# Moving VectorE's product of aggregate and x, and tying it to GpSimd's first scatter, in a graph kernel

## The chip, the cores and the metric

The kernel runs on one core of a Trainium2 chip, as one launch. The metric is the device time of the whole program in microseconds. The engines are named as the profile names them: PE (TensorE), DVE (VectorE), ACT (ScalarE), POOL (GpSimd) and SP (SyncE, which here only issues transfers).

## What is computed

Two graph layers run over 100,000 nodes of 64 features and 50,000 edges sorted by destination, each with a residual and a layer norm.

```
def L0(x):   messages = x[src] * edge_weight[:, None]
             agg = segment_sum(messages, dst, N)
             out = leaky(x * agg @ W1 + b1) + leaky(agg @ W2 + b2)      # leaky: slope 0.2
             return out * rsqrt(max(sum(out * out), 1e-12))
def L1(x):   messages = ffn(x[dst]; W1p, b1p, W2p, b2p) * edge_weight[:, None]
             agg = segment_sum(messages, src, N)
             out = ffn([x, agg]; W1u, b1u, W2u, b2u)                    # ffn: two layers, each with an exact gelu
             return out * rsqrt(max(sum(out * out), 1e-12))
x = layernorm(x + L0(x)); x = layernorm(x + L1(x))
```

## The kernel before

The work is done in three blocks, one after another: `first_edges`, `second_edges` and `last_rows`. The change is in the second.

The first block gathers x by source, weighs and joins the messages, and adds them into a table in device memory. A row of this table holds aggregate, x and centred x of a node.

The second block runs 98 rounds for nodes and edges together. In a round it takes one chunk of 1024 nodes (8 rows of 64 features in each partition), and one window of 512 edges (4 further rows, gathered from the table by destination). All 12 rows of a partition lie in one tile, `box`, of which there are six. DVE's `multiply` (L731) forms x times aggregate in place: both inputs are slices of `box` in SBUF, 128 partitions by 768 numbers. PE turns the rows (L570) and multiplies by the weights (L579), ACT writes the sloped branch (L658), and DVE's `leak` (L737) takes the larger branch, in three steps q = 0, 1, 2 for each chunk. PE's `outputs` (L589) forms the centred outputs, ACT squares them (L664), DVE sums the squares (L746), takes inverse roots by a chain of short instructions (L754 to L768), scales (L772) and adds the rows (`add_rows`, L780). ACT squares the sum (L669), DVE sums those squares (`sum_centred`, L742), and one round later DVE normalizes (L785). The neighbour rows then go through the message network on PE and ACT. PE's `join` (L625) weighs and sums the messages of a window, and ACT's `take` (L691) copies them into one of three tiles `ms`.

POOL does nothing in this block but issue indirect transfers. For each window k it issues four scatters, which add `ms` into `state` in device memory (L546), and then four gathers of window k + 8 into `box` (L532). Scatter k waits until window k is taken and until all four transfers of scatter k - 1 have landed. `take` of window i waits until the scatters of window i - 3 have landed, because they read the same `ms` tile. A gather of window i waits until `add_rows` has released the tile `box` of window i - 6.

SP issues, once a round, the load of the next chunk (768 KB, after `add_rows` has released its tile), the load of the join weights (640 KB) and the store of a finished chunk (256 KB), in that order.

Each engine has its own order, written out by hand as a loop over rounds t. `of(t, lag, f)` calls f for index t - lag. DVE's order, with ACT's lags one higher for the same index, is the one that matters:

```
for t in range(ROUNDS):
    of(t, 2, sum_outputs)
    ...
    of(t, 1, leak, 1)
    of(t, 2, add_rows)
    of(t, 1, leak, 2)
    of(t, 2, sum_centred)
    of(t, 0, multiply)
```

DVE's instructions start in this order and none passes another.

Of the kernel before, what the change touches and what calls it, by code (L numbers as in the profile page):

```python
# [28 lines left out]
def wait(eng, sem, n):  # L29

    if n > 0:
        eng.wait_ge(sem, n)  # L32
# [7 lines left out]
def gnn_kernel(nc, x, src, dst, edge_weight, w1a, w2a, b1a, b2a, w1p, b1p, w2p, b2p, w1u, b1u, w2u, b2u, out):  # L40
# [42 lines left out]
    with ctx:  # L83
# [6 lines left out]
        def sem(name, c=ctx):  # L90
            return c.enter_context(nc.semaphore(name))
# [350 lines left out]
        def second_edges():  # L442
            c = ExitStack()
            with c:
# [28 lines left out]
                scattered = [sem(f"scattered1_{h}") for h in range(HALVES)]  # L473
# [3 lines left out]
                    "squared", "summed_o", "squared_y", "summed_y", "guarded", "chain", "scaled", "added", "normed", "spread"))  # L477
                nt_up, nt_in, mixed, gelu1, mixed2, gelu2, summed, taken, preset = (sem(f"{q}1") for q in (
                    "nt_up", "nt_in", "mixed", "gelu1", "mixed2", "gelu2", "summed", "taken", "preset"))
                ROUNDS = NWIN + 6  # L480
                SPARE = R // 2 * M8

# [10 lines left out]
                with nc.Block(no_gpsimd_drain=True) as block:  # L493
                    @block.sync
                    def _(sp):
                        def load(i):

                            s = i % SB
                            wait(sp, added, i - SB + 1)
                            rows, p, g = chunk(table_rows, i)  # L500
                            sp.dma_start(box[s][0:p, WT:WT + g, :, :].rearrange("p g a f -> p g (a f)"),
                                         rows.rearrange("(g p) f -> p g f", g=g)).then_inc(loaded[s], 16)

                        def load_join(i):
                            wait(sp, summed, i - SW + 1)
                            sp.dma_start(weigh[i % SW][:, :].rearrange("p (b f) -> p b f", f=P), joins[i].rearrange("b p f -> p b f")).then_inc(joined[i % SW], 16)

                        def store(i):
                            sp.wait_ge(normed, i + 1)
                            rows, p, g = chunk(state_rows[:, 0, :], i)  # L510
                            sp.dma_start(rows.rearrange("(g p) f -> p g f", g=g), y[i % SY][0:p, WT:WT + g, :]
                                         ).then_inc(stored[i % SY], 16)

                        for i in range(NWIN + 7):
                            if i < NWIN:
                                load(i)
                            if 0 <= i - 6 < NWIN:
                                load_join(i - 6)
                            if 0 <= i - 7 < NWIN:
                                store(i - 7)  # L520
                        for s in range(SY):
                            sp.wait_ge(stored[s], 16 * lies(NWIN, s, SY))

                    @block.gpsimd
                    def _(pool):
                        def gather(i, h):

                            if h == 0:
                                wait(pool, added, i - SB + 1)
                            for b in range(JOIN * h, JOIN * (h + 1)):  # L530
                                at = i * WT + b
                                pool.indirect_dma_start(out=box[i % SB][:, b, :, :].rearrange("p a f -> p (a f)"), out_offset=None,  # L532
                                                        in_=table_rows[:, :],
                                                        in_offset=bass.IndirectOffsetOnAxis(ap=node[1][:, at:at + 1], axis=0),
                                                        ).then_inc(gathered[i % SB], 16)

                        def scatter(k, h):

                            if h == 0:
                                pool.wait_ge(taken, k + 1)  # L540
                                wait(pool, scattered[HALVES - 1], 16 * JOIN * k)
                            else:
                                pool.wait_ge(scattered[h - 1], 16 * JOIN * (k + 1))
                            for b in range(JOIN * h, JOIN * (h + 1)):
                                at = k * WT + b
                                pool.indirect_dma_start(out=state[:, :], out_offset=bass.IndirectOffsetOnAxis(ap=sidx[1][:, at:at + 1], axis=0),  # L546
                                                        in_=ms[k % SM][:, b, :], in_offset=None, compute_op=ALU.add,
                                                        ).then_inc(scattered[h], 16)

                        for i in range(LEAD):  # L550
                            for h in range(HALVES):
                                gather(i, h)
                        for k in range(NWIN):
                            for h in range(HALVES):
                                scatter(k, h)
                                if k + LEAD < NWIN:
                                    gather(k + LEAD, h)
                        for h in range(HALVES):
                            pool.wait_ge(scattered[h], 16 * JOIN * NWIN)

                    @block.tensor
                    def _(pe):
# [66 lines left out]
                        def of(t, lag, what, *more):  # L629
                            if 0 <= t - lag < NWIN:  # L630
                                what(t - lag, *more)

                        for t in range(ROUNDS):
                            of(t, 2, products, 2)
# [13 lines left out]
                    def _(act):  # L648
# [45 lines left out]
                        def of(t, lag, what, *more):  # L694
                            if 0 <= t - lag < NWIN:
                                what(t - lag, *more)
# [3 lines left out]
                        act.wait_ge(preset, 1)  # L700
                        for t in range(ROUNDS):
                            of(t, 5, second_gelu)
# [13 lines left out]
                    def _(dve):  # L716
# [16 lines left out]
                        def leak(i, q):  # L733

                            n = 3 * i + q
                            dve.wait_ge(sloped, n + 1)
                            dve.scalar_tensor_tensor(out=leaky[i % 2][q][:, :], in0=z_p[n % 2][:, :], scalar=bz[:, 0:1],  # L737
                                                     in1=leaky[i % 2][q][:, :], op0=ALU.add, op1=ALU.max).then_inc(leaked, 1)
# [48 lines left out]
                        def of(t, lag, what, *more):  # L787
                            if 0 <= t - lag < NWIN:
                                what(t - lag, *more)

                        for t in range(ROUNDS):
                            of(t, 2, sum_outputs)
                            if 2 <= t < NWIN + 3:
                                roots(t)
                            of(t, 1, leak, 0)
                            of(t, 3, normalize)
                            of(t, 2, scale)
                            of(t, 1, leak, 1)
                            of(t, 2, add_rows)
                            of(t, 1, leak, 2)  # L800
                            of(t, 2, sum_centred)
                            of(t, 0, multiply)

        def last_rows():
            c = ExitStack()
# [210 lines left out]

        first_edges()
        second_edges()
        last_rows()

# [22 lines left out]
```

## Time and profile before

| | |
|---|---|
| median of 3 runs | 2975.88 us (2974.57 to 2979.17) |
| the profiled execution's own time | 2982.28 us |
| its span, first to last instruction | 2980.5 us |
| mean granted TensorE clock | 0.767 |
| busy in the span | PE 2150.9 us, DVE 2211.5, ACT 1070.7, POOL 2361.0 |
| POOL's scatters of the second block (L546) | 392, 630.8 us busy |
| POOL's gathers of the second block (L532) | 392, 401.9 us busy |

The three runs are executions without the profiler. Durations come from one profiled execution, whose own time is 6.4 us above the median. Busy time is what an engine spends in instructions. Issuing instructions of SP and ACT, waits and branches don't count, but POOL's indirect transfers do, since GpSimd works out their descriptors.

### The profile page before, as it was taken

The numbers are of one execution on the slowest core, as the hardware profiler recorded it, in microseconds if no ns is written. First come the engines' busy times: TensorE is split into PE (matmuls) and PEld (weight loads), VectorE is DVE, ScalarE is ACT, GpSimd is POOL, SyncE is SP. The second block draws the span as 40 slices with busy tenths as digits, with TensorE's granted clock in tenths as the row PEclk, the third lists the DMA queues.
The fourth block names the chain that finished last, engine by engine and source line by source line (L and its number), as shares of the span: only waits on it lengthen the run. The fifth ranks groups of instructions, "written<-read, shape, count | busy, mean of one in ns | idle before, by whom it ended". The sixth has DMA issues, their size and how long they took to land. (4 is left out here: it accounts for less than half of the span.)

```text
span 2980.5 us, 39234 instructions
## 1 busy us (share of the span) xinstructions
PE 2150.9 (72%) x11956; PEld 1675.4 (56%) x11956; DVE 2211.5 (74%) x5627; ACT 1070.7 (36%) x1964; POOL 2361.0 (79%) x1774
## 2 busy tenths in 40 slices
PE   4036555555555554269999999989999998599997
PEld 3035555555554544247777666666666666366664
DVE  5079888888888886457778777777777777188888
ACT  0000000000000000035555455545555554288887
POOL 7777888888888888758888888888888887488888
PEclk8555555555555555579999999999999999699998
DMA  9998888888888767467787777777777776356664
GB/s 228 206 204 187 180 173 177 175 183 177 176 180 170 158 141 151 83 175 179 186 187 184 169 166 176 180 176 159 178 178 169 170 175 123 79 196 207 206 209 156
DMA packets 1036087, 516.48 MB, mean 173 GB/s; under 512 B 540544, under 2 KB 998336, under 8 KB 1035880
## 3 DMA queue, kind: packets, MB, share of 16 engines
q1 hardware_dynamic: 764616, 372.57, 47.6%
q0 software_dynamic: 144256, 77.17, 19.2%
q10 hardware_dynamic: 127008, 64.23, 7.6%
q8 instruction: 99, 1.62, 0.2%
q14 instruction: 108, 0.88, 0.1%
HBM read 269.97 MB, written 243.84 MB: 172 GB/s over the span
## 5 line engine op out<-in xcount | busy, mean ns | idle before, releaser
L300 PE MATMUL sums<-xg,weigh 128*128 128x64 f32 x1960 | 437.7, 420 | 514.8 <-ACT ms L323 358.7
L546 POOL DMA_INDIRECT state<-ms,sidx x392 | 630.8, 1609 | 145.2 <-issue 116.9
L256 POOL DMA_INDIRECT table<-ms,sidx x392 | 622.2, 1587 | 142.2 <-issue 115.5
L300 PEld LDWEIGHTS sums<-xg,weigh 128*128 128x128 f32 x1960 | 423.2, 329 | 548.6 <-issue 471.5
L368 DVE TENSOR_SCALAR weigh<-rowp,key,ew 128x128 f32<-128x128 f32 (+3 forms) x784 | 423.9, 602 | 167.9 <-PE rowp L288 160.7
L532 POOL DMA_INDIRECT box<-table,node_dst x392 | 401.9, 1025 | 130.0 <-issue 107.6
L243 POOL DMA_INDIRECT xg<-in_x,node_src x392 | 382.8, 976 | 120.8 <-issue 104.9
L323 ACT ACTIVATE ms<-sums 128x256 f32<-128x256 f32 x98 | 37.6, 384 | 1144.4 <-DMA table<-ms,sidx 1076.1
L374 DVE SCALAR_TENSOR_TENSOR seen<-rowp,key,earlier 128x128 f32<-128x128 f32 (+3 forms) x784 | 383.1, 544 | 0.0
L579 PE MATMUL z_p<-turned_s,wz 128*128 128x512 f32 x588 | 331.7, 647 | 24.9 <-ACT turned_s L652 20.8
L589 PE MATMUL o_p<-cenz,leaky 128*128 128x65 f32 x2352 | 285.1, 278 | 27.6 <-DVE leaky L737 27.2
L589 PEld LDWEIGHTS o_p<-cenz,leaky 128*128 128x128 f32 x2352 | 272.9, 193 | 48.3 <-DVE leaky L737 48.2
L288 PE MATMUL rowp<-ident,key 128*128 128x128 f32 x784 | 186.4, 418 | 129.2 <-DVE seen L374 122.0
L625 PEld LDWEIGHTS ffo<-g,weigh_in 128*128 128x128 f32 x1960 | 238.3, 195 | 48.0 <-issue 47.3
L658 ACT ACTIVATE leaky<-z_p,bz 128x512 f32<-128x512 f32 x294 | 202.0, 687 | 129.6 <-PE z_p L579 119.3
L288 PEld LDWEIGHTS rowp<-ident,key 128*128 128x128 f32 x784 | 166.8, 241 | 129.9 <-DVE seen L374 122.8
L625 PE MATMUL ffo<-g,weigh_in 128*128 128x64 f32 x1960 | 234.4, 276 | 1.6 <-issue 1.6
L737 DVE SCALAR_TENSOR_TENSOR leaky<-z_p,bz,leaky 128x512 f32<-128x512 f32 x294 | 217.9, 741 | 21.6 <-ACT leaky L658 21.3
L570 PEld LDWEIGHTS turned_p<-ident,box 128*128 128x128 f32 x1176 | 154.6, 155 | 131.5 <-issue 80.3
L870 POOL TENSOR_TENSOR inv<-ssq,mhalf 128x8 f32<-128x8 f32 x98 | 161.0, 1642 | 74.4 <-DVE ssq L975 74.4
L570 PE MATMUL turned_p<-ident,box 128*128 128x128 f32 x1176 | 180.9, 296 | 48.0 <-DVE box L731 48.0
L742 DVE TENSOR_REDUCE v<-sq_y 128x12 f32<-128x768 f32 x98 | 93.4, 953 | 157.5 <-ACT sq_y L669 157.5
(94 smaller groups left out, 3549.6 us busy)
## 6 DMA issues: line engine op xcount, KB each, us to landing
box<-table SPq DMA_DIRECT2D x97, 768.0 KB, 5.3
joins<-weigh ACTq DMA_DIRECT2D x98, 640.0 KB, 3.8
weigh_in<-joins SPq DMA_DIRECT2D x98, 640.0 KB
table<-rows SPq DMA_DIRECT2D x97, 512.0 KB, 5.4
pair<-state SPq DMA_DIRECT2D x97, 512.0 KB, 3.8
xin<-in_x SPq DMA_DIRECT2D x97, 256.0 KB, 6.1
state<-y SPq DMA_DIRECT2D x97, 256.0 KB, 7.7
out<-y SPq DMA_DIRECT2D x97, 256.0 KB, 2.2
```

The lines of the kernel that those rows point to most:

```text
L243: pool.indirect_dma_start(out=xg[:, i, :], out_offset=None, in_=x[:, :], in_offset=bass.IndirectOffsetOnAxis(ap=node[0][:, i:i + 1], axis= ...
L256: pool.indirect_dma_start(out=table[:, :], out_offset=bass.IndirectOffsetOnAxis(ap=sidx[0][:, i:i + 1], axis=0), in_=ms[k % MR][:, b, :], ...
L288: last = pe.transpose(rowp[n][k % 2][:, b * P:(b + 1) * P], key[n][:, i:i + 1].to_broadcast([P, P]), ident[:, :])
L300: last = pe.matmul(sums[k % 2][:, a * D:(a + 1) * D], block_of(0, k, b)[:, a * P:(a + 1) * P], xg[:, k * WT + b, :], start=b == a, stop=b ...
L368: last = dve.tensor_scalar(block_of(n, k, b), rowp[n][k % 2][:, (b + 1 - m) * P:(b + 1) * P], key[n][:, i:i + 1], ew[:, i:i + 1], ALU.is_e ...
L374: last = dve.scalar_tensor_tensor(out=seen[b][:, 0:m * P], in0=rowp[n][k % 2][:, (b + 1 - m) * P:(b + 1) * P], scalar=key[n][:, i:i + 1], ...
L532: pool.indirect_dma_start(out=box[i % SB][:, b, :, :].rearrange("p a f -> p (a f)"), out_offset=None, in_=table_rows[:, :], in_offset=bass ...
L546: pool.indirect_dma_start(out=state[:, :], out_offset=bass.IndirectOffsetOnAxis(ap=sidx[1][:, at:at + 1], axis=0), in_=ms[k % SM][:, b, :] ...
L570: last = pe.transpose(turned_p[n % 2][:, g * P:(g + 1) * P], box[i % SB][:, 4 * q + g, 0:2, :].rearrange("p a f -> p (a f)"), ident[:, :])
L579: pe.matmul(z_p[n % 2][:, :], wz[:, :], turned_s[q][:, :], start=True, stop=True).then_inc(z_up, 1)
L589: last = pe.matmul(o_p[:, b, g * M8:(g + 1) * M8], leaky[i % 2][r // 4][:, r % 4 * P:(r % 4 + 1) * P], cenz[:, :], start=True, stop=True)
L625: last = pe.matmul(ffo[:, (WT + a) * D:(WT + a + 1) * D], weigh[i % SW][:, at * P:(at + 1) * P], g2[i % 2][:, b * D:(b + 1) * D], start=b ...
```

## The change

A new semaphore `begun` is raised by POOL itself when it has finished the instruction of the first scatter of a window. The semaphore `scattered` is raised by the transfer when its data have landed, and stays as it was. DVE's third leaky step of chunk i waits until `begun` is at least i - 4, which is when the first scatters of windows 0 to i - 5 have been worked out. The product `multiply` of the next chunk now follows this leaky step directly, ahead of `sum_centred`.

```diff
+                begun = sem("begun1")
...
                                 pool.indirect_dma_start(out=state[:, :], out_offset=bass.IndirectOffsetOnAxis(ap=sidx[1][:, at:at + 1], axis=0),
                                                         in_=ms[k % SM][:, b, :], in_offset=None, compute_op=ALU.add,
-                                                        ).then_inc(scattered[h], 16)
+                                                        engine_sem=begun if b == 0 else None).then_inc(scattered[h], 16)
...
                         def leak(i, q):
 
                             n = 3 * i + q
+                            if q == 2:
+                                wait(dve, begun, i - 4)
                             dve.wait_ge(sloped, n + 1)
...
                             of(t, 1, leak, 2)
+                            of(t, 0, multiply)
                             of(t, 2, sum_centred)
-                            of(t, 0, multiply)
```

## Rows read from the trace of the kernel before

**Rows 1.** Busy time of each engine in one stretch, windows 18 to 88

```profile
core 0: us, PE busy (x) PEld busy (x) DVE busy (x) ACT busy (x) POOL busy (x), PEclk, DMA share, GB/s
...
1568.00:2490.00 922.00, 846.97 (x5151) 631.82 (x5150) 687.59 (x1568) 470.67 (x856) 748.46 (x569) 0.95 0.76 173
```

**Rows 2.** The page's costliest groups: busy us, mean ns, idle before and releaser

```profile
L546 POOL DMA_INDIRECT state<-ms,sidx x392 | 630.8, 1609 | 145.2 <-issue 116.9
...
L532 POOL DMA_INDIRECT box<-table,node_dst x392 | 401.9, 1025 | 130.0 <-issue 107.6
...
L742 DVE TENSOR_REDUCE v<-sq_y 128x12 f32<-128x768 f32 x98 | 93.4, 953 | 157.5 <-ACT sq_y L669 157.5
```

**Rows 3.** Timeline of POOL over three windows: start us, us, operation, idle before

```profile
2100.50 2.22 POOL L546 DMA_INDIRECT state<-ms,sidx  x1 [0.30 <-issue]
...
2112.51 1.62 POOL L532 DMA_INDIRECT box<-table,node_dst  x1 [0.30 <-issue]
...
2125.84 1.28 POOL L532 DMA_INDIRECT box<-table,node_dst  x1 [0.30 <-issue]
2127.43 1.62 POOL L546 DMA_INDIRECT state<-ms,sidx  x1 [0.30 <-issue]
2129.36 1.57 POOL L546 DMA_INDIRECT state<-ms,sidx  x1 [0.30 <-issue]
...
2138.83 0.95 POOL L532 DMA_INDIRECT box<-table,node_dst  x1 [0.30 <-issue]
2140.08 1.63 POOL L546 DMA_INDIRECT state<-ms,sidx  x1 [0.30 <-issue]
```

**Rows 4.** Timeline of DVE over the same windows

```profile
2100.27 0.95 DVE L731 TENSOR_TENSOR box<-box 128x768 f32<-128x768 f32 x1
...
2110.06 0.74 DVE L737 SCALAR_TENSOR_TENSOR leaky<-z_p,bz,leaky 128x512 f32<-128x512 f32 x1
2111.49 0.95 DVE L742 TENSOR_REDUCE v<-sq_y 128x12 f32<-128x768 f32 x1 [0.70 <-ACT sq_y L669]
2112.36 0.95 DVE L731 TENSOR_TENSOR box<-box 128x768 f32<-128x768 f32 x1
...
2122.01 0.74 DVE L737 SCALAR_TENSOR_TENSOR leaky<-z_p,bz,leaky 128x512 f32<-128x512 f32 x1
...
2125.36 0.95 DVE L731 TENSOR_TENSOR box<-box 128x768 f32<-128x768 f32 x1
...
2140.18 0.95 DVE L731 TENSOR_TENSOR box<-box 128x768 f32<-128x768 f32 x1
```

**Rows 5.** All products L731: duration ns min/median/max, first and last start

```profile
L731 DVE TENSOR_TENSOR box<-box x98: 946/948/1001, 1283.1 to 2515.2; 128x768 f32<-128x768 f32 x98
```

**Rows 6.** Timeline of POOL: first scatters of windows 0, 18, 19 and 89

```profile
1331.50 1.62 POOL L546 DMA_INDIRECT state<-ms,sidx  x1 [9.14 <-ACT ms L691]
...
1568.11 1.62 POOL L546 DMA_INDIRECT state<-ms,sidx  x1 [1.17 <-DMA state<-ms,sidx]
...
1580.78 1.63 POOL L546 DMA_INDIRECT state<-ms,sidx  x1 [0.30 <-issue]
...
2489.92 2.23 POOL L546 DMA_INDIRECT state<-ms,sidx  x1 [0.30 <-issue]
```

**Rows 7.** Timeline of DVE: third leaky steps of chunks 23 and 24

```profile
1570.14 0.74 DVE L737 SCALAR_TENSOR_TENSOR leaky<-z_p,bz,leaky 128x512 f32<-128x512 f32 x1
...
1582.10 0.74 DVE L737 SCALAR_TENSOR_TENSOR leaky<-z_p,bz,leaky 128x512 f32<-128x512 f32 x1
```

**Rows 8.** Timeline of POOL at the block's end: first scatters of windows 91 and 97

```profile
2513.81 1.55 POOL L546 DMA_INDIRECT state<-ms,sidx  x1 [3.37 <-ACT ms L691]
...
2571.15 1.55 POOL L546 DMA_INDIRECT state<-ms,sidx  x1 [2.40 <-DMA state<-ms,sidx]
```

**Rows 9.** Timeline of ACT: the last take, window 97

```profile
2555.09 0.38 ACT L691 ACTIVATE ms<-ffo 128x256 f32<-128x256 f32 x1 [4.64 <-DMA state<-ms,sidx]
```

**Rows 10.** Timeline of the span's last us: DVE waiting for POOL

```profile
2973.42 3.61 POOL L876 TENSOR_TENSOR rstd<-var,mhalf 128x8 f32<-128x8 f32 x2 [0.46 <-DVE var L1000]
...
2977.06 0.69 DVE L1006 TENSOR_TENSOR y<-y,rstd 128x512 f32<-128x512 f32 x1 [0.91 <-POOL rstd L876]
```

## The prediction

> **What bounds the kernel now.** The chain of work that ended last runs almost wholly through the third block, so it says little here. I went to the busy time of each engine in the stretch of the second block in which all is in swing, from the first scatter of window 18 to that of window 89. There POOL is busy 748.46 of 922 us with 569 instructions, PE 846.97, DVE 687.59 [rows 1]. POOL's share looks like slack and is none: ahead of nearly every one of its instructions stands the same 0.30 us put down to "issue" [rows 2, 3], and 569 x 0.30 = 171 us; 748 + 171 = 919 us. POOL has no free time in this stretch. PE is busier by its busy time but runs at POOL's pace: when nothing holds DVE, its loop with PE and ACT turns in 2122.01 - 2110.06 = 11.95 us [rows 4], while the stretch took (2489.92 - 1568.11) / 71 = 12.98 us a window [rows 6].
>
> Next, what a window costs POOL. Window 61 goes from 2127.43 to 2140.08, 12.65 us [rows 3], and I take it as a clean one. The windows before it cost more because single instructions are long: a scatter of 2.22 us beside 1.62, a gather of 1.62 and another of 1.28 us beside 0.95 [rows 3]. Laid beside DVE's timeline, each long one starts while the product L731 runs. The product of 2100.27 ends at 2101.22 and the scatter that starts at 2100.50 is 0.60 long; product 2112.36, gather 2112.51: 0.67 long; product 2125.36, gather 2125.84: 0.33 long [rows 3, 4]. All three fit one reading: POOL wants something in SBUF at its start and gets it about 0.14 us before the recorded end of the product (2101.22 - 2100.50 - 0.60 = 0.12; 0.13; 0.14). The product of 2140.18 starts 0.10 us after a scatter did, and that scatter takes 1.63 us, as usual [rows 3, 4]. So only POOL's start is exposed. DVE pays nothing: over 98 products the longest is 1001 ns [rows 5]. I laid every product of the block on every start of POOL in this way; 67 starts lie inside a product and are 30.4 us too long together, and all other starts, under any other instruction of DVE, are regular to 0.03 us. The page agrees roughly: a clean window has scatters of 6.32 and gathers of 3.90 us, 98 of each are 619 and 382 us, and the page has 630.8 and 401.9 [rows 2], 31 us more.
>
> **The change part by part.** The product moved ahead of `sum_centred`. Before, DVE stood 0.70 us for ACT's squares between leaky step and `sum_centred` (157.5 us over 98 rounds [rows 2, 4]). The product now fills this, but the next thing on DVE, the sum of PE's new outputs, still waits for leaky step, PE and ACT, and the loop of 11.95 us goes through these. So I cost this at nothing, neither gained nor lost, as DVE isn't the bound. Its cover is 12.65 - 11.95 = 0.70 us a window; without it a delay would count fully.
>
> The wait for `begun`. Call C the end of POOL's first scatter of a window. In the free start of the block, DVE gains some 1.2 us a window on POOL (windows 0 to 17 took POOL (1568.11 - 1331.50) / 18 = 13.14 us [rows 6]). The third leaky step that is to wait for window 18 started at 1570.14, 0.41 us after C (1568.11 + 1.62); that for window 19 at 1582.10, 0.31 before C (1580.78 + 1.63) [rows 6, 7]. So the wait binds from about window 19, and then in every window, since 11.95 is less than 12.65. Until then, nothing is locked and the product meets POOL's starts at chance; its hits in windows 0 to 17 come to about 8 us before, and laying the product 0.66 us behind each leaky step of the same rows gives about 7 us. I count 1 us gained.
>
> From window 19 on, the leaky step starts at C + d, the product at C + d + 0.66 (recorded times overlap by 0.08 us: L742 lasts 0.95 and the next starts 2112.36 - 2111.49 = 0.87 behind it [rows 4]; so 0.74 gives 0.66). POOL starts its second scatter at C + 0.31 (2129.36 - 2127.43 - 1.62) and its third 1.87 later, at C + 2.18 [rows 3]. A product does no harm if it starts after the first and at least 0.81 us (0.95 - 0.14) before the second: between C + 0.31 and C + 1.37, so for d from -0.35 to 0.71. The trace has no such completion of an indirect transfer. The nearest row is DVE waiting for POOL's arithmetic in the last us: POOL ends at 2973.42 + 3.61 = 2977.03, DVE starts at 2977.06, d = 0.03 [rows 10]. From above, POOL's own next instruction follows 0.30 us after an end, which would bound d by about 0.4. Both ends lie inside. I take 0.1: product from C + 0.76 to C + 1.71, with 0.4 us of room on either side. No start is hit.
>
> What this is worth: the 71 windows from 18 to 88 took 921.8 us; at 12.65 they take 898.2. That is 23.6 us [rows 3, 6]. The hit of 0.61 us on window 89 goes too. With the first part, 25 us. The upper end is all hits, 30; the lower end has the clean windows at 12.72, 71 x 0.07 = 5 us less, so 20.
>
> What `begun` costs POOL. There is no row for this either. Below: the arithmetic L876, which raises a semaphore, runs back to back (3.61 us for two with 1.68 each otherwise), so nothing. Above: another gap of 0.30 us in each of 98 windows, 29 us. I take nothing, as the semaphore travels with an instruction that is there already.
>
> What is queued behind the waiting leaky step: product, both sums, the roots, scale, add. PE's outputs and so SP's loads start later against POOL. Two places could notice. First, ACT's take of window k + 3 needs the scatters of window k; it now comes about 12.6 us after C, and the last scatter's instruction ends at C + 5.6 (6.32 - 1.62 + 3 x 0.30), so the ring of three `ms` tiles no longer holds ACT up; its waits turn into waits of DVE for `begun`, at no cost. Second, the end of the block, where POOL has only scatters and DVE's chain could come last. Take 97 was at 2555.09 and its scatter at 2571.15 [rows 8, 9]: 16 us of room. Before, leaky steps ran ahead of C, by 7.0 us in window 61 (2122.01 against 2127.43 + 1.62 [rows 3, 4]) and by 8 at most; they will run 0.1 behind, so the room shrinks to 8 us at least. POOL there waits for the landing of its own scatters (2.40 us [rows 8]), and stays the bound. Nothing lost.
>
> On the port the Trainium skill speaks in two places of "SBUF — State Buffer". Its section "Who interferes with whom" says that a VectorE instruction with two SBUF inputs contends with a GpSimd instruction that reads SBUF; the rows agree, with 0.60 us on a scatter. But it also says that whoever issues first holds the pair for its whole instruction and the other fully blocks. That speaks against this change, since the product would then be held inside the second scatter; what it would give is the last rival below.
>
> **The rivals.** Late landing, the one that ends slower. Scatter k + 1 may not start before scatter k has landed, and the landing is late when SP's loads, which follow `add_rows`, run at the same time as the scatters. Window 18 started 1.17 us after the instruction ahead instead of 0.30, for the landing of 17 [rows 6]. There the leaky step was 2.0 us behind C, near where it will now be locked. Against it: one window on, with the step 0.41 behind C, the gap is 0.30 and the window took 12.67 us [rows 6, 7], and this is nearer to 0.1. The room from the last scatter's end to the next window is 12.65 - 1.62 - 5.6 = 5.4 us. If landing took 0.87 beyond it each time, it would cost 71 x 0.87 = 62 us: 62 - 25 = 37 slower, 3013. It decides from 0.35 us a window; at 0.5 the time is 2986. Chance 0.10, spread over these.
>
> The lock misses: d lies above 0.71 or below -0.35, or the semaphore costs POOL 0.30. Then hits or gaps of about 0.3 us a window stay, as many as before: 2970 to 2980. For it speaks that neither was ever seen in this trace. A d of 1.4 would give a hit of up to 0.7 in each window and end slower. Chance 0.10, of which 0.03 is slower.
>
> Half of it: the lock holds but is often late, as PE or ACT make a loop longer than 12.65, or landings delay some windows. 2958 to 2968. The free loop's steadiness speaks against it. Chance 0.10.
>
> Held inside: the product waits until the second scatter ends at C + 1.88, ends at C + 2.83 and delays the third by 0.5 us in each window, 71 x 0.5 = 36 us, less 25: 2987. The 1001 ns of the longest product [rows 5] and the product at 2140.18 speak against it. The second sentence of the skill's section is this rule. Chance 0.02.
>
> **How the numbers follow.** The forecast, 20 to 30 us gained, has 0.68. Against its own profiled execution the kernel would go from 2982.3 to 2957; the sum taken from the median, 2975.9 - 25 = 2951, is the prediction, and 2946 to 2956 its own range. To leave out no more than 2 in 10 the range takes in the half and stops short of the rest: 2943 to 2970. A change within 0.2% (6 us) can't be told from none. Faster by more: 0.68 + 0.10 + 0.01 = 0.79. Within: 0.08. Slower: 0.13, from late landing, the missed lock and the held product.
>
> **What would show it.** POOL's windows from about 19 on at 12.65 us with all scatters at 1.55 to 1.63; L546 and L532 near 623 and 388 us busy; the product 0.3 to 0.6 us behind the start of a second scatter; idle time of DVE ahead of the third leaky step, about 0.7 us, put down to POOL; ACT's long waits ahead of L691 gone. It is wrong if first scatters show gaps above 0.30 us for a landing, if products or second scatters grow, or if the first scatter is followed by a longer gap.

## The result and the profile after

The changed kernel takes 2969.47 us (2966.56 to 2972.94) beside 2977.64 us of the kernel before: ratio 0.9974 [0.9967, 0.9981]. It is 8 us faster; the forecast was 25. Its profiled execution took 2972.03 us, 10.3 us below that of before, so the profile shows a little more gain than the unprofiled runs. Their medians differ by 8.2 us; single executions of the kernel before spread over 12 us (2972.83 to 2984.79), so the 2 us between the two gains are within it. Mean granted clock is 0.759, 0.767 before.

The lines have moved: scatter L547, gather L533, product L732, leaky step L740, `sum_centred` L745, `sum_outputs` L749. From the page (busy us, mean ns, idle before and releaser), to lay beside [rows 2]:

```profile
L547 POOL DMA_INDIRECT state<-ms,sidx x392 | 630.6, 1609 | 152.6 <-issue 117.3
...
L533 POOL DMA_INDIRECT box<-table,node_dst x392 | 386.5, 986 | 130.1 <-issue 113.4
...
L590 PE MATMUL o_p<-cenz,leaky 128*128 128x65 f32 x2352 | 318.6, 298 | 51.5 <-DVE leaky L740 51.5
...
L749 DVE TENSOR_REDUCE v<-sq_o 128x12 f32<-128x780 f32 x98 | 94.7, 966 | 234.5 <-ACT sq_o L665 234.5
L740 DVE SCALAR_TENSOR_TENSOR leaky<-z_p,bz,leaky 128x512 f32<-128x512 f32 x294 | 218.3, 743 | 28.6 <-DMA state<-ms,sidx 19.1
```

Gathers are at the forecast (386.5 us, 388 was given): they are hardly hit any more. Scatters are as dear as before, where 623 was forecast. The last row has the new wait. Its releaser is named as the landing of the scatters, but the instruction waits for `begun`, which POOL raises itself; the profile doesn't tell the two apart. PE's row is one that the forecast did not have: PE is now idle 51.5 us ahead of `outputs`, for the leaky step, and the same matmuls are busy for 318.6 us. Before, they had:

```profile
L589 PE MATMUL o_p<-cenz,leaky 128*128 128x65 f32 x2352 | 285.1, 278 | 27.6 <-DVE leaky L737 27.2
```

POOL's first scatters of windows 18, 60, 61, 89 and 97, with the second and third of 60 and 61 (start, us, idle before), to lay beside [rows 3, 6]:

```profile
1567.77 1.62 POOL L547 DMA_INDIRECT state<-ms,sidx  x1 [0.30 <-issue]
...
2105.96 1.62 POOL L547 DMA_INDIRECT state<-ms,sidx  x1 [0.30 <-issue]
2107.88 1.58 POOL L547 DMA_INDIRECT state<-ms,sidx  x1 [0.30 <-issue]
2109.76 1.56 POOL L547 DMA_INDIRECT state<-ms,sidx  x1 [0.30 <-issue]
...
2118.60 1.62 POOL L547 DMA_INDIRECT state<-ms,sidx  x1 [0.30 <-issue]
2120.52 1.57 POOL L547 DMA_INDIRECT state<-ms,sidx  x1 [0.30 <-issue]
2122.40 2.23 POOL L547 DMA_INDIRECT state<-ms,sidx  x1 [0.30 <-issue]
...
2478.00 1.62 POOL L547 DMA_INDIRECT state<-ms,sidx  x1 [0.30 <-issue]
...
2561.29 1.55 POOL L547 DMA_INDIRECT state<-ms,sidx  x1 [2.35 <-DMA state<-ms,sidx]
```

Window 60, from 2105.96 to 2118.60, took 12.64 us with no start delayed: the clean window of the forecast. In the next the third scatter takes 2.23 us. Windows 18 to 88 together took 2478.00 - 1567.77 = 910.2 us, where 898.2 was forecast and 921.8 measured before. Laid on each other as in the prediction, products and starts of POOL give 15 hits (starts of POOL inside a product, which grow longer by it) in these windows, 8.9 us (46 and 22.4 us before); waits for a landing beyond the usual 0.30 us give 2.8 us more (1.2 before). 898.2 + 8.9 + 2.8 = 909.9, so both together account for the stretch.

DVE at the same place:

```profile
2107.61 0.75 DVE L740 SCALAR_TENSOR_TENSOR leaky<-z_p,bz,leaky 128x512 f32<-128x512 f32 x1 [0.62 <-DMA state<-ms,sidx]
2108.28 0.95 DVE L732 TENSOR_TENSOR box<-box 128x768 f32<-128x768 f32 x1
...
2114.00 0.97 DVE L749 TENSOR_REDUCE v<-sq_o 128x12 f32<-128x780 f32 x1 [3.91 <-ACT sq_o L665]
...
2121.60 0.74 DVE L740 SCALAR_TENSOR_TENSOR leaky<-z_p,bz,leaky 128x512 f32<-128x512 f32 x1
2122.26 0.95 DVE L732 TENSOR_TENSOR box<-box 128x768 f32<-128x768 f32 x1
```

The first leaky step starts 0.03 us after POOL's first scatter ends (2105.96 + 1.62 = 2107.58), and the product 0.40 us into the second scatter: both as forecast. The next leaky step comes 2121.60 - 2107.61 = 13.99 us later, without a wait for POOL, and the product behind it starts at 2122.26 and is running when the third scatter starts, at 2122.40. DVE was late, and it was late because of a wait of 3.91 us for ACT's squares, which waited for PE:

```profile
2071.31 2.79 PE L590 MATMUL o_p<-cenz,leaky 128*128 128x65 f32 x24
...
2083.30 2.89 PE L590 MATMUL o_p<-cenz,leaky 128*128 128x65 f32 x24 [0.32 <-DVE leaky L740]
...
2095.76 2.89 PE L590 MATMUL o_p<-cenz,leaky 128*128 128x65 f32 x24 [0.83 <-DVE leaky L740]
...
2108.42 4.69 PE L590 MATMUL o_p<-cenz,leaky 128*128 128x65 f32 x24 [1.03 <-DVE leaky L740]
```

The 24 matmuls of `outputs` took 4.69 us instead of 2.89. The busy time of three stretches says why (PE, PEld, DVE, ACT, POOL busy, then the granted clock as a share of full speed, DMA share, GB/s):

```profile
core 0: us, PE busy (x) PEld busy (x) DVE busy (x) ACT busy (x) POOL busy (x), PEclk, DMA share, GB/s
...
1568.00:2490.00 922.00, 868.92 (x5171) 670.45 (x5170) 688.16 (x1582) 473.00 (x862) 743.95 (x576) 0.93 0.75 174
...
2106.00:2109.00 3.00, 1.97 (x18) 1.74 (x18) 2.38 (x4) 1.39 (x3) 2.69 (x2) 1.00 0.31 62
2109.00:2116.00 7.00, 7.00 (x32) 6.48 (x32) 2.96 (x9) 1.87 (x4) 5.57 (x5) 0.51 1.10 265
2116.00:2119.00 3.00, 3.00 (x12) 1.38 (x12) 2.68 (x10) 2.27 (x4) 2.29 (x3) 0.99 0.26 71
```

For 7 us TensorE ran at half its clock, 1.2 GHz instead of 2.4, from 0.8 us after it had stood 1.03 us ahead of `outputs`. The granted clock of windows 18 to 88 has 19 such falls, 17 of them 6.8 us long and two 3.4, at 1583.5, 1634.5, 1686.0 and so on, about every fourth window. Before there were 13, about every fifth window, and each lay where ACT and DVE were held for the ring of `ms` tiles, with PE idle for 1.8 to 3.6 us. They cost nothing there: POOL's instructions went on 0.30 us apart. Now DVE has no such time in hand.

The falls come in a cycle, which the four rows of PE show. After a fall DVE is 1.4 us late, doesn't wait for `begun` at all and catches up 0.7 us or more a window, so PE's idle time ahead of `outputs` grows window by window: 0, 0.32, 0.83 and 1.03 us, and then comes the next fall. Seventeen of the 19 falls begin 0.5 to 1.2 us behind the end of such an idle time of 1.01 to 1.05 us, and the two short ones 2.6 us behind one of 1.01 and one of 1.42. An idle time of this length is not always enough: the windows at 1839.83 and 2365.71 had 1.04 and 1.08 us and no fall.

### The profile page after: what moved, and what is told of

It reads as the page before. It is cut to its first block and busy times, and to the rows that moved or that the text cites. A ratio compares the mean times of both kernels' runs of the same rounds, so it can differ in the third digit from the quotient of the medians.

```text
span 2970.2 us, 39327 instructions
## 1 busy us (share of the span) xinstructions
PE 2166.3 (73%) x11956; PEld 1709.2 (58%) x11956; DVE 2205.7 (74%) x5627; ACT 1069.6 (36%) x1964; POOL 2345.2 (79%) x1774
## 3 DMA queue, kind: packets, MB, share of 16 engines
q8 instruction: 99, 1.62, 0.2%
## 5 line engine op out<-in xcount | busy, mean ns | idle before, releaser
L547 POOL DMA_INDIRECT state<-ms,sidx x392 | 630.6, 1609 | 152.6 <-issue 117.3
L533 POOL DMA_INDIRECT box<-table,node_dst x392 | 386.5, 986 | 130.1 <-issue 113.4
L590 PE MATMUL o_p<-cenz,leaky 128*128 128x65 f32 x2352 | 318.6, 298 | 51.5 <-DVE leaky L740 51.5
L590 PEld LDWEIGHTS o_p<-cenz,leaky 128*128 128x128 f32 x2352 | 305.7, 212 | 71.5 <-DVE leaky L740 71.4
L580 PE MATMUL z_p<-turned_s,wz 128*128 128x512 f32 x588 | 322.9, 631 | 22.7 <-ACT turned_s L653 19.0
L749 DVE TENSOR_REDUCE v<-sq_o 128x12 f32<-128x780 f32 x98 | 94.7, 966 | 234.5 <-ACT sq_o L665 234.5
L740 DVE SCALAR_TENSOR_TENSOR leaky<-z_p,bz,leaky 128x512 f32<-128x512 f32 x294 | 218.3, 743 | 28.6 <-DMA state<-ms,sidx 19.1
```

Source lines behind the costliest of these rows:

```text
L580: pe.matmul(z_p[n % 2][:, :], wz[:, :], turned_s[q][:, :], start=True, stop=True).then_inc(z_up, 1)
L590: last = pe.matmul(o_p[:, b, g * M8:(g + 1) * M8], leaky[i % 2][r // 4][:, r % 4 * P:(r % 4 + 1) * P], cenz[:, :], start=True, stop=True)
```

## The experiments

"Mid" is the time of windows 18 to 88 in the profile, hits are starts of POOL inside a product there with the us that they add, landing is what waits for a landing add beyond 0.30 us, and falls are falls of the clock that begin there.

| kernel | median us | beside before's | ratio | mid us | hits | landing us | falls |
|---|---|---|---|---|---|---|---|
| before | 2977.64 | | | 921.8 | 46 / 22.4 | 1.2 | 13 |
| after | 2969.47 | 2977.64 | 0.9974 [0.9967, 0.9981] | 910.2 | 15 / 8.9 | 2.8 | 19 |
| e1_move_only | 2979.74 | 2977.33 | 1.0010 [1.0001, 1.0019] | 921.8 | 48 / 23.6 | 0.8 | 18 |
| e2_gate_only | 2975.48 | 2977.33 | 1.0000 [0.9991, 1.0009] | 913.7 | 30 / 11.4 | 5.2 | 20 |
| e3_fill3 | 2957.22 | 2977.33 | 0.9934 [0.9921, 0.9947] | 900.8 | 2 / 1.0 | 1.7 | 0 |
| e4_gate_at_sum | 2954.58 | 2977.33 | 0.9926 [0.9913, 0.9938] | 899.0 | 1 / 0.8 | 1.3 | 2 short |
| e5_gate_at_leak0 | 3021.22 | 3002.52 | 1.0069 [1.0051, 1.0086] | 929.8 | 35 / 15.4 | 13.6 | 5 |
| e6_fill1 | 3028.16 | 3002.52 | 1.0084 [1.0069, 1.0098] | 937.2 | 29 / 12.7 | 25.4 | 10 |
| e7_before_fill3 | 3007.20 | 3002.52 | 1.0015 [1.0005, 1.0025] | 917.3 | 71 / 14.4 | 4.9 | 0 |
| e8_gate_at_sum_tight | 3007.32 | 3002.52 | 1.0023 [1.0007, 1.0039] | 920.0 | 69 / 19.5 | 1.3 | 0 |
| f1_change_again | 2970.45 | 2978.39 | 0.9973 [0.9962, 0.9983] | 908.6 | 16 / 8.6 | 1.4 | 18 |
| f2_gate_at_sum | 2952.31 | 2978.39 | 0.9915 [0.9901, 0.9929] | 898.6 | 1 / 0.3 | 1.0 | 2 short |
| f3_gate_at_leak0 | 3023.68 | 2978.39 | 1.0144 [1.0129, 1.0160] | 958.0 | 28 / 15.7 | 44.9 | 12 |
| f4_fill1 | 2968.37 | 2978.39 | 0.9969 [0.9957, 0.9981] | 906.6 | 13 / 5.9 | 2.3 | 17 |

**e1_move_only.** The product moved, without `begun`. Diff to after:

```diff
-                                                        engine_sem=begun if b == 0 else None).then_inc(scattered[h], 16)
+                                                        ).then_inc(scattered[h], 16)
...
-                            if q == 2:
-                                wait(dve, begun, i - 4)
```

> The product alone is moved ahead of sum_centred; there is no semaphore begun and no wait for it. Theory (the wait is what gains, by locking the product between two starts of GpSimd, and PE's clock falls take half of it back): nothing is locked here, the product meets GpSimd's starts at chance. Laying a product 0.66 us behind each leaky step of the rows of before gives about 33 us of hits against 30: ratio 0.999 to 1.003 (0 to 8 us slower), scatters and gathers of the block together near 1033 us busy. Rival (the move gains, since it fills VectorE's wait of 0.70 us a window): ratio near 0.997, as in the whole change.

The mid stretch is that of before to the tenth, with about as many hits. Moving the product alone gains nothing. The 18 falls here, 14 of them 3.4 us long, show that falls don't need the wait for `begun`: they lie, as before, at idle times of PE of 1.6 to 3.2 us for the ring of `ms` tiles, and cost as little.

**e2_gate_only.** The wait kept, the product back behind `sum_centred`:

```diff
-                            of(t, 0, multiply)
                             of(t, 2, sum_centred)
+                            of(t, 0, multiply)
```

> The wait for begun ahead of the third leaky step stays, the product is back behind sum_centred. Theory: in a locked window the product starts about 1.6 us behind the end of the first scatter, ends 0.2 to 0.25 us too late for the third scatter's start, and lengthens it by that in about three windows of four: some 12 us of hits, besides the clock falls of the whole change. Ratio 0.997 to 0.9985. Rival (the wait is worth its gain wherever the product lies): ratio 0.9974 with hits no larger than in the whole change (8.9 us in windows 18 to 88).

Hits add 11.4 us, as expected, but the ratio, 1.0000, is worse than the expected 0.997 to 0.9985. The profiled execution (2971.96 us) was 3.5 us below the median of its kind, so its mid stretch flatters it. Neither the wait nor the position of the product is faster alone; the gain needs both.

**e3_fill3.** Three matmuls whose result nobody reads, ahead of `outputs`, so that TensorE stands less there:

```diff
+                        def fill(n):
+
+                            for _ in range(n):
+                                pe.matmul(turned_p[0][:, 0:D], ident[:, :], ident[:, 0:D], start=True, stop=True)
...
+                            if 2 <= t < NWIN + 2:
+                                fill(3)
```

> The whole change, and TensorE runs three matmuls of 128x64 without a use (into a turned_p bank that is free then) ahead of the outputs, in the time in which it waits for the leaky step. Theory (each of the 17 falls of the clock to half begins after TensorE stood 1.03 us for the leaky step, which the wait for begun holds up; the loop of 14.0 us that follows makes VectorE 1.4 us late and the product hits the third scatter): the idle time shrinks to about 0.3 us, no clock falls between window 18 and 88, no hits there, windows at 12.65 to 12.70 us, 9 to 11 us gained on the whole change: ratio 0.9935 to 0.9950. Rival (the clock falls for another reason, or the added matmuls make the loop longer than 12.65): falls every fourth window as before, ratio 0.997 or above.

The expectation came true but for the ratio, 0.9934, which lies just below its range. The gap ahead of `outputs` is now about 0.4 us in every locked window (0.44 at most), the clock does not fall once in the stretch, and 2 hits are left. Busy time of the stretch, then the timelines of PE, POOL and DVE in one window:

```profile
1568.00:2490.00 922.00, 876.49 (x5702) 681.07 (x5701) 698.81 (x1609) 482.70 (x878) 741.87 (x580) 1.00 0.75 175
```

```profile
2013.25 2.89 PE L595 MATMUL o_p<-cenz,leaky 128*128 128x65 f32 x24 [0.38 <-DVE leaky L747]
```

```profile
2010.79 1.62 POOL L547 DMA_INDIRECT state<-ms,sidx  x1 [0.30 <-issue]
2012.71 1.57 POOL L547 DMA_INDIRECT state<-ms,sidx  x1 [0.30 <-issue]
2014.59 1.55 POOL L547 DMA_INDIRECT state<-ms,sidx  x1 [0.30 <-issue]
```

```profile
2012.44 0.75 DVE L747 SCALAR_TENSOR_TENSOR leaky<-z_p,bz,leaky 128x512 f32<-128x512 f32 x1 [0.59 <-DMA state<-ms,sidx]
2013.11 0.95 DVE L739 TENSOR_TENSOR box<-box 128x768 f32<-128x768 f32 x1
```

DVE waits for `begun` as in the changed kernel, 0.59 us, and the product lies at the same place, 0.40 us into the second scatter. Only PE's gap and the clock differ, and 12 us of the changed kernel's 2969.5 go with them. The three matmuls shorten the gap and add work for PE at the same time; this run doesn't separate the two, but in e4, below, PE gets no added work and the falls are all but gone too.

**e4_gate_at_sum** and **f2_gate_at_sum**, one kernel in two comparisons. The wait stands one instruction later, ahead of `sum_centred`, so that the third leaky step and with it `outputs` are not held; the product follows `sum_centred`:

```diff
-                            if q == 2:
-                                wait(dve, begun, i - 4)
...
+                            wait(dve, begun, i - 3)
...
-                            of(t, 0, multiply)
                             of(t, 2, sum_centred)
+                            of(t, 0, multiply)
```

> The wait for begun stands ahead of sum_centred instead of the third leaky step, and the product is back behind sum_centred: leaky step, wait, sum_centred, product. TensorE's outputs are no longer held up by the wait. The product starts about 0.9 us behind the end of the first scatter, still between two starts. Theory: the idle time of TensorE in one piece ahead of the outputs is what brings the clock down; here it is spread or lies elsewhere, few or no falls, and even a product late by 1.35 us would start just behind the third scatter's start: hits under 3 us in windows 18 to 88, ratio 0.993 to 0.996. Rival (the idle time as a whole brings the clock down, wherever it lies): falls every fourth window, ratio 0.995 to 0.998.

> The wait ahead of sum_centred, leaky step, wait, sum_centred, product, as in the run that was fastest. On a chip of the first kind: ratio 0.9926 again (0.991 to 0.994). On one of the second kind: no lock, as the loop is not faster than GpSimd's window: ratio 1.000 to 1.003. Rival (it gains by something else than the lock): below 0.998 on either.

Windows take 12.66 us each and the kernel is 23 to 26 us faster than before, which is what the forecast gave the change; for e4 the expected 0.993 to 0.996 was too cautious by a little. Timelines of DVE, POOL and PE in one window, then the busy time of the stretch:

```profile
2068.90 0.74 DVE L738 SCALAR_TENSOR_TENSOR leaky<-z_p,bz,leaky 128x512 f32<-128x512 f32 x1
...
2072.15 0.95 DVE L745 TENSOR_REDUCE v<-sq_y 128x12 f32<-128x768 f32 x1 [2.50 <-DMA state<-ms,sidx]
2073.02 0.95 DVE L732 TENSOR_TENSOR box<-box 128x768 f32<-128x768 f32 x1
```

```profile
2070.49 1.62 POOL L547 DMA_INDIRECT state<-ms,sidx  x1 [0.30 <-issue]
2072.42 1.59 POOL L547 DMA_INDIRECT state<-ms,sidx  x1 [0.30 <-issue]
```

```profile
2074.11 1.06 PE L571 MATMUL turned_p<-ident,box 128*128 128x128 f32 x8 [1.03 <-DVE box L732]
```

```profile
1568.00:2490.00 922.00, 833.40 (x5271) 620.87 (x5269) 712.77 (x1608) 481.83 (x876) 743.16 (x581) 1.00 0.77 176
```

The leaky step runs 3.2 us ahead of the end of the first scatter (2070.49 + 1.62 = 2072.11), DVE waits 2.50 us behind it, and the product starts 0.91 us after that end. PE has a gap of 1.03 us here too, in 62 and 63 windows, ahead of turning, for the product, and is idle for 922.00 - 833.40 = 88.6 us of the stretch against 53.1 in the changed kernel; yet the mean clock is 1.00. The two short falls do begin at such a gap, 0.1 us behind its end, but some 60 like it pass. So neither the length of one gap nor the sum of idle time alone brings the clock down. Where in the round the gap lies matters, and how is left open.

**e5_gate_at_leak0, e6_fill1, e7_before_fill3, e8_gate_at_sum_tight.** These ran beside a kernel before that itself took 3002.52 us. There, ACT's squares of the outputs started 0.7 to 1 us later behind PE's outputs than in the other comparisons, DVE's loop was 12.8 to 12.9 us, longer than POOL's 12.65, and a lock can't hold. The parts that no kernel here changes were longer too: the block's first scatter started at 1347.87 us in e7 and at 1331.50 in the profile of the kernel before; the first block is the same in both. The cause is open. The expectation of f1 speaks of two kinds of chip, but the record gives one chip number (13) for these four and for f1 to f4. The four say little on the change: e5, e6 and e8 missed every range of their expectations, only e7 met one. Two were repeated (f3, f4, below).

e5 moves the wait to the first leaky step:

```diff
-                            if q == 2:
+                            if q == 0:
```

> The whole change, but the wait for begun stands ahead of the first leaky step (q = 0) instead of the third. The product then starts about 4.6 us behind the end of the first scatter, between the fourth scatter's start (4.06) and the first gather's (5.91 less 0.81). TensorE's idle time of about 1 us now lies ahead of the third product of chunk i - 1 (L580), no longer ahead of its outputs. Where the wait stood ahead of sum_centred, idle time of the same length (1.04 us, ahead of the turning) brought only two short falls of the clock, so length alone doesn't decide. Theory (only ahead of the outputs does such a gap bring the clock down): at most 3 falls in windows 18 to 88, ratio 0.992 to 0.9945. Rival (the place at the turning is the harmless one, any other brings falls): 12 falls or more, ratio 0.996 to 0.999.

e6 is e3 with `fill(1)` in place of `fill(3)`:

> The whole change with one matmul of 128x64 without a use ahead of the outputs, where there were three. It takes 0.24 us from the idle time of 1.03 us ahead of the outputs, and leaves about 0.8 us. Theory (the length of this gap decides; in the whole change windows with 0.83 us passed and the fall came in the next, with 1.03): few or no falls, ratio 0.993 to 0.995. Rival (it takes all three matmuls; a gap of 0.8 us in every window still adds up to a fall): falls go on, if farther apart, ratio 0.996 to 0.9975.

e7 is the kernel before with the three matmuls of e3:

> The kernel before, with the same three matmuls without a use ahead of the outputs and nothing else. Theory (the matmuls gain only where the wait for begun makes the lock and the clock breaks it): no lock, the product meets GpSimd's starts at chance, GpSimd stays the bound: ratio 0.998 to 1.002. The falls of the clock in the kernel before lie in windows where VectorE waits for the ring of ms tiles anyway. Rival (a steadier clock gains by itself): ratio 0.993 to 0.996, as with the whole change and three matmuls.

Filling alone is no gain here (1.0015), though the clock doesn't fall once in the stretch: 71 hits remain. That fits e3's gain not being that of the matmuls by themselves, but as this kernel ran under the other condition it doesn't show it. e8 is e4 with the tighter wait:

```diff
-                            wait(dve, begun, i - 3)
+                            wait(dve, begun, i - 2)
```

> The wait ahead of sum_centred, as in the run before that was fastest, but for one window later of GpSimd (begun at least i - 2 in place of i - 3), so that VectorE may run one window less ahead. The lock takes hold about 10 windows earlier, near window 9 instead of 19: hits and late landings of the first 18 windows (8.5 us) fall to 3 or 4. At the block's end VectorE's chain is 12.65 us later against GpSimd, and the room there is 8 to 12 us: 0 to 5 us lost. Theory (both are of one size): ratio 0.9905 to 0.9935. Rival (the end takes over and costs a whole window): ratio 0.994 to 0.997.

It was to show a lock one window tighter; no lock took hold, and the test is void. One thing stands on the side: where DVE's loop was longer than POOL's window, the three kernels with the wait were 0.2 to 0.8% slower than the kernel before.

**f1_change_again.** The changed kernel once more:

> The whole change once more, unaltered, as the measure for the three that run beside it. The four kernels before this call ran on a chip on which ScalarE's squares started about 1 us later behind TensorE's outputs, VectorE's loop took about 12.9 us and so was no faster than GpSimd's window, and the kernel before took 3002 us instead of 2977. If this call finds a chip of the first kind (kernel before near 2977): ratio 0.9974 again, about 17 falls of the clock between windows 18 and 88, one product in four on the third scatter. If it finds one of the second kind: the wait for begun never binds, no lock, ratio 1.000 to 1.008. Rival (the change gains on any chip): ratio 0.997 there too.

0.9973, with 18 falls and 16 hits: the falls and hits belong to the kernel and not to one execution.

**f3_gate_at_leak0.** The kernel of e5:

> The wait ahead of the first leaky step. Its first run fell on the chip of the second kind and told nothing of the question. On a chip of the first kind, as stated then: few falls of the clock if only a gap ahead of the outputs brings it down (ratio 0.992 to 0.9945); 12 falls or more if the turning is the only harmless place (0.996 to 0.999). On one of the second kind: 1.005 to 1.009 as measured there.

Timelines of POOL, DVE and SP's issues in one window:

```profile
2101.34 1.55 POOL L547 DMA_INDIRECT state<-ms,sidx  x1 [0.31 <-issue]
2103.20 1.02 POOL L533 DMA_INDIRECT box<-table,node_dst  x1 [0.30 <-issue]
...
2110.23 1.62 POOL L547 DMA_INDIRECT state<-ms,sidx  x1 [2.21 <-DMA state<-ms,sidx]
```

```profile
2097.34 0.75 DVE L740 SCALAR_TENSOR_TENSOR leaky<-z_p,bz,leaky 128x512 f32<-128x512 f32 x1 [1.60 <-DMA state<-ms,sidx]
...
2101.91 0.95 DVE L732 TENSOR_TENSOR box<-box 128x768 f32<-128x768 f32 x1
```

```profile
2101.37 0.36 SPq L502 DMA_DIRECT2D box<-table  x1
```

The product, from 2101.91 to 2102.86, lies between the starts of the last scatter (2101.34) and of a gather (2103.20), as calculated. But now SP's load of 768 KB is issued at 2101.37, as the last scatter of the window starts, and the next window's first scatter waits 2.21 us for the landing. Over the stretch 35 such waits beyond 0.30 us add 44.9 us. Laid side by side from window 19 on, they fall apart cleanly: in 34 windows the load was issued within 0.05 us of the last scatter's start, and the next scatter waited 0.9 to 2.2 us beyond 0.30 in all of them; in the 36 others it was issued 1.1 us or more later, and none waited. This is the rival late landing, with the product some 4 us later against POOL than in the change. At 1.0144 the kernel is 45 us slower than before, outside both ranges of the expectation, which had not thought of the load. The clock falls 12 times here as well, for 10 to 17 us each, although PE has no more than its usual 0.32 us ahead of `outputs`. Each fall lies in or within 1.9 us behind an idle time of PE of 1.5 to 2.8 us ahead of the third product (L580), so the narrower theory that only the gap ahead of `outputs` brings falls is refuted.

**f4_fill1.** The kernel of e6, one matmul instead of three:

> One matmul without a use ahead of the outputs. On a chip of the first kind, as stated before its first run: few falls of the clock if the length of the gap ahead of the outputs decides (0.8 us instead of 1.03; ratio 0.993 to 0.995), falls that go on, farther apart, if it takes all three matmuls (0.996 to 0.9975). On one of the second kind: 1.006 to 1.010 as measured there.

PE ahead of `outputs`, part of its 24 matmuls:

```profile
1898.14 2.09 PE L595 MATMUL o_p<-cenz,leaky 128*128 128x65 f32 x11 [0.85 <-DVE leaky L747]
```

All 24 took 4.87 us. The gap is still 0.85 us and 17 falls go on; the ratio, 0.9969, is in the range of the expectation's rival. One matmul is too little: e3's gain came with a gap of 0.4 us.

## Why the forecast was half wrong

**The hits.** Right. A product that is running when an instruction of POOL starts costs it up to 0.7 us; windows without one take 12.65 us, in the changed kernel as in e3 and e4.

**The move.** Costed at nothing; right (e1).

**`begun`.** d was taken as 0.1 us and is 0.03, the lower bound from [rows 10]. It costs POOL nothing: the gap behind the first scatter is 0.30 us as ever. Where the lock holds, the product lay where it was put, 0.70 us after C, the end of the first scatter. Right.

**The lock and its cover.** This step failed. The prediction said that the wait binds "in every window, since 11.95 is less than 12.65", called the difference of 0.70 us the cover, and let ring waits turn into waits for `begun` "at no cost". Both loop times were right. What was put at nothing is what the wait does to PE. DVE's wait of 0.62 us is handed on to PE, which stands 1.03 us ahead of `outputs` instead of 0.32, and this idle time is not free: the clock falls, the next `outputs` takes 1.80 us longer, that loop is 13.99 instead of 12.65 us, and the product is 13.99 - 12.64 = 1.35 us late, over the third start. Such hits are 8.9 us of the 12.0 missing in windows 18 to 88. That the falls make the hits is shown by e3, where both are gone with the wait and the product in place, and e4 shows that the wait as such is harmless when `outputs` doesn't hang on it. That the length of the gap makes the falls is well supported (0.4 us none, up to 0.9 us 17 falls, up to 1.03 us and more 18 and 19) but not shown apart from its place, and e3's matmuls also add work.

**The rest of the sum.** Landings took 2.8 us of the stretch, 1.2 before. In windows 0 to 17 the forecast had 1 us gained and 0.1 was lost: hits fell from 7.4 to 6.0 us, but landing waits rose from 0.4 to 3.1. At the end 0.6 was to be gained and 2.1 us were lost (83.29 us from window 89 to 97 instead of 81.23): landings 17.0 instead of 15.3 us, hits 1.35 instead of 0.9. The block starts 0.5 us earlier. 11.6 - 0.1 - 2.1 + 0.5 = 9.9 us, against 10.3 between the profiled executions.

**The rivals.** "Half of it" is what happened: a lock that holds but is often late as PE makes a loop longer than 12.65. Its time of 2958 to 2968 ends just below what was measured, and it was given a chance of 0.10, on the ground that the free loop is steady; but that loop was read without the wait in it. Late landing is real (f3) but not at this phase. The lock didn't miss, and "held inside" is refuted: products inside a second scatter take 0.95 us, and third scatters behind them are regular.

**What the profile could have told.** The kernel before had the sign: its 13 falls each lay at an idle time of PE, behind a wait for the ring. One of them lasted from 2074.58 to 2081.41; these are PE's two matmuls of the same kind inside it and one round later:

```profile
2075.37 1.22 PE L605 MATMUL ffn<-nt_s,wp 128*128 128x256 f32 x2 [2.72 <-ACT nt_s L674]
...
2089.49 0.65 PE L605 MATMUL ffn<-nt_s,wp 128*128 128x256 f32 x2
```

The granted clock laid beside the waits would have shown that a wait handed on to PE can bring a fall and that matmuls then take nearly twice as long. `outputs` takes 2.89 us at full clock, so a fall on it could add more than the 0.70 us by which 11.95 is below 12.65. That an idle time of only 1.03 us is enough was not to be seen there: the shortest that had a fall was 1.8 us.

**Left open.** What it is in the gap's place in the round that brings the clock down, and why the whole kernel ran longer, with ACT starting later, in one set of runs.

## What to carry to other kernels

A wait that ties a fast engine to a slow one can stand at several places with the same effect on the slow one: try its neighbours and read TensorE's clock at each. One instruction later, the same lock gained 23 to 26 us instead of 8; ahead of the first leaky step, it lost 45. Check the loop's margin not only in its free time but with TensorE at half its clock for one round. A lock fixes the phase of everything behind it, so look up which transfers it places beside which landings.

## What the runs showed of the hardware

- A product on VectorE with both inputs in SBUF isn't slowed by an indirect transfer that GpSimd is working out: 0.95 us from 2108.28 to 2109.23, wholly inside a scatter of 1.58 us. Only GpSimd's start is held, up to about 0.14 us before the product's end. The Trainium skill, "SBUF — State Buffer", section "SBUF: two separate sides", says that of a VectorE instruction with two SBUF inputs and a GpSimd instruction that reads SBUF, the one that starts first gets the shared ports for the whole instruction and the other fully blocks. Where the product starts first the runs agree but for those 0.14 us; where the scatter starts first they differ, as the product isn't held at all.
- GpSimd's own completion of an indirect transfer reached VectorE 0.03 us after the recorded end and added nothing to GpSimd's gap of 0.30 us.
- TensorE's granted clock fell to half behind idle times of about 1 us. With gaps ahead of `outputs` that grew to 1.03 us it fell 19 times in 71 windows, mostly for 6.8 us; with up to 0.9 us (f4) 17 times; with 0.4 us in every locked window (e3) never. With 1.03 us ahead of turning in nearly every window it fell twice, for 3.4 us (e4, f2).
- With a load of 768 KB issued within 0.05 us of the start of a window's last scatter, GpSimd waited 0.9 to 2.2 us beyond its usual 0.30 for the landing, in 34 of 34 windows; with the load 1.1 us or more later, in none of 36 (f3).
